# Expert stage of a vision tower kernel: both expert products in two row tiles of 64

## The reference

```
logits = x @ Wr.T                       # 16 experts
top_p, top_idx = top_k(softmax(logits), 2)
for each expert e:
    h   = gelu(x @ W1[e] + b1[e])       # 192 -> 768, "up"
    out = h @ W2[e] + b2[e]             # 768 -> 192, "down"
    y  += gate[e] * out
return x + y
```

## Time and profile before

| | us |
|---|---|
| median of 3 runs | 836.96 (836.1 to 840.61) |
| span of the profiled execution, first to last instruction | 860.4 |
| busy in it: PE | 726.7 |
| PEld | 609.2 |
| DVE | 408.3 |
| ACT | 371.2 |
| POOL | 348.5 |

### The profile page before, as it was taken

How to read it: one execution, slowest core, us unless ns; L and a number is a source line. 1 busy time by engine, 2 the same in 40 slices (tenths; PEclk the granted TensorE clock), 3 DMA queues, 4 the chain that set the end, 5 groups by cost and what they waited for, 6 DMA issues and landing times.

```text
span 860.4 us, 18555 instructions
## 1 busy us (share of the span) xinstructions
PE 726.7 (84%) x5774; PEld 609.2 (71%) x5774; DVE 408.3 (47%) x1214; ACT 371.2 (43%) x890; POOL 348.5 (41%) x534
## 2 busy tenths in 40 slices
PE   0409479999999999999853899999999999999990
PEld 0307356777677767676632799999999999999980
DVE  7001144688888888888765233222222222222228
ACT  0103225676666666666621333333333333333344
POOL 7740212357777777777675022122212212221220
PEclk9999558999999999999975899999999999999995
DMA  7710654444445544544061492645698778588249
GB/s 192 127 14 19 196 120 111 104 94 124 122 121 129 125 121 122 125 118 124 31 214 49 128 303 85 199 122 152 195 303 263 220 224 250 182 244 248 60 144 328
DMA packets 117226, 132.31 MB, mean 154 GB/s; under 512 B 18081, under 2 KB 102050, under 8 KB 116834
## 3 DMA queue, kind: packets, MB, share of 16 engines
q1 hardware_dynamic: 108434, 111.06, 46.9%
q0 software_dynamic: 8720, 20.36, 7.6%
HBM read 147.30 MB, written 35.49 MB: 212 GB/s over the span
## 4 chain that ended last, share of the span: by engine, by line
PE 58%; DVE 12%; issue 11%; POOL 9%; another core or an unknown queue 4%; ACT 2%; DMA 1%; SPq 1%; POOLq 1%; DVEq 0%; ACTq 0%
PE BK L451 18%; PE BK L436 13%; PE BK L441 8%; PE BK L707 4%; POOL slot_rows L1609 3%; PE BK L426 2%; PE BK L792 2%; PE BK L833 2%; POOL rs L1558 2%; DVE negmax L1322 2%; PE BK L812 2%; POOL hr L1598 1%; DVE hr L574 1%; PE BK L759 1%
## 5 line engine op out<-in xcount | busy, mean ns | idle before, releaser
L473 ACT ACTIVATE pixels<-BK,b1t 128x128 f32<-128x128 f32 x474 | 131.2, 375 | 241.8 <-PE BK L441 241.8
L585 POOL DMA_INDIRECT pair_rows<-shared x79 | 76.0, 962 | 294.0 <-DVE shared L551 289.5
L451 PE MATMUL BK<-shared,pixels 128*128 128x192 f32 x948 | 167.9, 325 | 0.0
L451 PEld LDWEIGHTS BK<-shared,pixels 128*128 128x128 f32 x948 | 153.0, 189 | 0.1
L1322 DVE TENSOR_REDUCE negmax<-BK 128x6 f32<-128x1536 f32 x64 | 112.5, 1757 | 25.0 <-PE BK L812 22.5
L436 PE MATMUL BK<-shared 128*128 128x128 f32 x948 | 120.0, 277 | 1.9 <-DVE shared L544 1.9
L436 PEld LDWEIGHTS BK<-shared 128*128 128x128 f32 x948 | 117.0, 193 | 2.8 <-DVE shared L544 2.8
L540 DVE TENSOR_TENSOR shared<-shared 128x1 int32<-128x1 f32 x79 | 12.6, 160 | 177.8 <-PE BK L427 175.6
L1113 ACT ACTIVATE shared<-BK 128x1536 f32<-128x1536 f32 x64 | 92.7, 1449 | 7.6 <-PE BK L833 6.7
L1609 POOL DMA_INDIRECT slot_rows<-xr,adr x64 | 64.8, 1013 | 36.5 <-issue 13.7
L441 PE MATMUL BK<-shared 64*128 64x128 f32 x948 | 74.9, 291 | 0.0
(11 more groups left out here) (202 smaller groups left out, 1087.9 us busy)
## 6 DMA issues: line engine op xcount, KB each, us to landing
shared<-ew SPq DMA_DIRECT2D x82, 576.0 KB
shared<-ew SPq DMA_DIRECT2D x82, 384.0 KB
shared<-up_rest SPq DMA_DIRECT2D x82, 192.0 KB
shared<-qk_parts SPq DMA_DIRECT2D x112, 96.0 KB
shared<-slot_rows SPq DMA_DIRECT2D x79, 104.0 KB
shared<-eb SPq DMA_DIRECT2D x82, 96.0 KB
qk_parts<-shared SPq DMA_DIRECT2D x32, 192.0 KB, 2.0
shared<-qk_parts SPq DMA_DIRECT2D x16, 288.0 KB
```

The source lines that it names most:

```text
L451: last = nc.tensor.matmul(Y[p], hT[p][:, c * P:(c + 1) * P], w2b[w][:, c, :], start=(c == 0), stop=(c == FC - 1))
L473: last = nc.scalar.activation(hT[p][:, c * P:(c + 1) * P], H[p][c], ACT.Gelu, bias=b1t[:, c, t:t + 1])
L585: nc.gpsimd.indirect_dma_start(pair_d, bass.IndirectOffsetOnAxis(t_dst[:, t:t + 1], 0), ysum[t % NB][:, :], None).then_inc(s[f"m_sc{t % NB ...
```

## The change

All PE work of the expert stage now uses 64 rows of the array at a time, alternating between the lower half (partitions 0 to 63, `LO`) and the upper half (`HI`).

- **Rows.** `rows_T` is four transposes of 64 rows by 128 features (features 0 to 127 and 64 to 191, for each half of the tile's rows) into two PSUM banks, one for each half of the array. The two banks now serve every tile, where before two tiles took turns. DVE copies them in three copies, the first of them 256 columns wide, so that the features lie in three slabs of 64: in the order 0, 1, 2 on the lower partitions and 1, 2, 0 on the upper ones.
- **Up.** The lower half of the array makes hidden chunks 0 to 2, the upper half chunks 3 to 5, each over three slabs: 18 products of 64 rows.
- **Down.** Each chunk of 128 hidden units is two products of 64 rows, the lower half summed in one PSUM bank and the upper in another: 12 products. DVE adds the bank of the lower half and the bias, waits for that, then adds the bank of the upper half. These two banks, too, serve every tile.
- **Weights.** The up weights are loaded straight from the input as two DMAs of 64 partitions x 3 slabs x 384. `st_up`, `up_rest` and the wait for them are gone.

```diff
 def rows_T(t):                                    # PE
-    p, r = t % 2, t % NB
+    r = t % NB
     pe.wait_ge(s[f"m_x{r}"], 16 * (t // NB) + 16)
-    wait_prev(pe, s["m_xT"], t - 1)
-    nc.tensor.matmul(XT[p][:, 0:P], xt[r][:, 0:P], ident[:, :], start=True, stop=True, is_transpose=True)
-    nc.tensor.matmul(XT[p][0:KR, P:2 * P], xt[r][:, P:E], ident[:, :],
-                     start=True, stop=True, is_transpose=True).then_inc(s["m_tr"], 1)
+    wait_prev(pe, s["m_xT"], t)
+    for f in range(2):
+        for h, k in enumerate((LO, HI)):
+            last = nc.tensor.matmul(XT[:, h, f, :], xt[r][k, f * RT:f * RT + P], ident[k, k],
+                                    start=True, stop=True, is_transpose=True)
+    last.then_inc(s["m_tr"], 1)
...
 def up(t):
-    for c in range(FC):
-        nc.tensor.matmul(H[p][c], w1a[w][:, c * P:(c + 1) * P], xtT[p][:, 0, :],
-                         start=(c % HC == 0), stop=False, skip_group_check=True)
     for c in range(HC):
-        for h in range(2):
-            k = slice(h * KR, (h + 1) * KR)
-            last = nc.tensor.matmul(H[p][h * HC + c], w1c[w][k, c * P:(c + 1) * P], xtT[p][k, 1, :],
-                                    start=False, stop=True, skip_group_check=True)
+        for k in range(NK):
+            for h, rows in enumerate((LO, HI)):
+                last = nc.tensor.matmul(H[p][h * HC + c], w1h[w][rows, (k + h) % NK, c * P:(c + 1) * P],
+                                        xtT[p][rows, k, :], start=(c == 0 and k == 0), stop=(k == NK - 1),
+                                        skip_group_check=True)
...
 def down(t):
-    wait_prev(pe, s["m_y"], t - 1)
+    wait_prev(pe, s["m_y"], t)
     for c in range(FC):
-        last = nc.tensor.matmul(Y[p], hT[p][:, c * P:(c + 1) * P], w2b[w][:, c, :],
-                                start=(c == 0), stop=(c == FC - 1))
+        for h, rows in enumerate((LO, HI)):
+            last = nc.tensor.matmul(Y[h], hT[p][rows, c * P:(c + 1) * P], w2b[w][rows, c, :],
+                                    start=(c == 0), stop=(c == FC - 1))
...
 def rows_T(t):                                    # DVE
-    V.tensor_copy(xtT[p][:, 0, :], XT[p][:, 0:P])
-    V.tensor_copy(xtT[p][0:KR, 1, :], XT[p][0:KR, P:2 * P])
-    V.tensor_copy(xtT[p][KR:P, 1, :], XT[p][0:KR, P:2 * P]).then_inc(s["m_xT"], 1)
+    V.tensor_copy(xtT[p][:, 0:2, :].rearrange("p s (h t) -> p s h t", h=2),
+                  XT[:, :, :, :].rearrange("p h s t -> p s h t"))
+    V.tensor_copy(xtT[p][LO, 2, :].rearrange("p (h t) -> p h t", h=2), XT[HI, :, 1, :])
+    V.tensor_copy(xtT[p][HI, 2, :].rearrange("p (h t) -> p h t", h=2), XT[LO, :, 0, :]) \
+        .then_inc(s["m_xT"], 1)
...
 def biased(t):
-    V.tensor_tensor(ysum[r][:, :], Y[p], b2b[w][:, :], ALU.add).then_inc(s["m_y"], 1)
+    V.tensor_tensor(ysum[r][:, :], Y[0], b2b[w][:, :], ALU.add).then_inc(s["m_yl"], 1)
+    dve.wait_ge(s["m_yl"], t + 1)
+    V.tensor_tensor(ysum[r][:, :], Y[1], ysum[r][:, :], ALU.add).then_inc(s["m_y"], 1)
...
 def first(t, e, new):                             # SP
-    sp.dma_start(w1a[w][:, :], ew1[ds(e, 1), 0:P, :].rearrange("a k f -> (a k) f"), cond=new) \
-        .then_inc(s[f"m_wa{w}"], 16)
-    sp.dma_start(w1c[w][:, :], w1c_d[ds(e, 1), :, :].rearrange("a k f -> (a k) f"), cond=new) \
-        .then_inc(s[f"m_wa{w}"], 16)
+    for h in range(2):
+        sp.dma_start(w1h[w][h * RT:(h + 1) * RT, :, :],
+                     ew1[ds(e, 1), :, h * (FF // 2):(h + 1) * (FF // 2)].rearrange("a (k r) f -> r (a k) f", r=RT),
+                     cond=new) \
+            .then_inc(s[f"m_wa{w}"], 16)
...
 def moe_loads(sp):
-    sp.wait_ge(s["st_w1c"], 32 * NE)
...
-            def st_up(e):
```

More of the change, by code:

```diff
@@ L69, in vit_tower @@
     qk_d = nc.dram_tensor("qk_parts", (2, 2, NPART, E, T), bf16).ap()
-    KR, HC = E - P, FC // 2
-    w1c_d = nc.dram_tensor("up_rest", (NE, P, FF // 2), fp32).ap()
+    RT, HC, NK = P // 2, FC // 2, 2 * E // P
+    assert NK * RT == E and NK == 3
     NW = 3
@@ L252, in vit_tower @@
         r_new = late([P, NTILE], i32)
-        w1a = [late([P, FF]) for w in range(NW)]
-        w1c = [late([P, FF // 2]) for w in range(NW)]
+        w1h = [late([P, NK, FF // 2]) for w in range(NW)]
         w2b = [late([P, FC, E]) for w in range(NW)]
@@ L260, in vit_tower @@
         t_dst = late([P, NTILE], i32)
-        xtT = [late([P, 2, P]) for p in range(2)]
+        xtT = [late([P, NK, P]) for p in range(2)]
         after_onehot = carve(pixels, n_pixels)
@@ L272, in vit_tower @@
         H = [[BK[:, 2 * p + c // HC, c % HC * P:(c % HC + 1) * P] for c in range(FC)] for p in range(2)]
-        XT = [BK[:, 4 + p, :] for p in range(2)]
-        Y = [BK[:, 6 + p, 0:E] for p in range(2)]
+        LO, HI = slice(0, RT), slice(RT, P)
+        XT = BK[:, 4:6, 0:P].rearrange("p h (s t) -> p h s t", s=2)
+        Y = [BK[:, 6 + h, 0:E] for h in range(2)]
         names = ("ld_const ld_idx0 ld_idx1 ld_idx2 ga0 ga1 ga2 dve_init pool_init act_xs "
@@ L282, in vit_tower @@
                  "r_dve r_diagd pe_row pe_tot r_tab "
-                 "m_x0 m_x1 m_x2 m_x3 m_wa0 m_wa1 m_wa2 m_wb0 m_wb1 m_wb2 m_b0 m_b1 m_b2 m_tr m_xT m_s1 m_gelu m_s2 m_y "
+                 "m_x0 m_x1 m_x2 m_x3 m_wa0 m_wa1 m_wa2 m_wb0 m_wb1 m_wb2 m_b0 m_b1 m_b2 m_tr m_xT m_s1 m_gelu m_s2 m_yl m_y "
                  "m_sc0 m_sc1 m_sc2 m_sc3 ld_p0 ld_p1 ld_p2 ld_p3 ld_p4 ld_p5 ld_p6 ld_p7 c_first c_out c_gated "
-                 "out_done st_w1c ld_b1 pe_b1 dve_b1 r_hot").split()
+                 "out_done ld_b1 pe_b1 dve_b1 r_hot").split()
         s = {n: sem(n) for n in names}
@@ L541, in rows_T @@
                 wait_prev(dve, s["m_s1"], t - 1)
-                V.tensor_copy(xtT[p][:, 0, :], XT[p][:, 0:P])
-                V.tensor_copy(xtT[p][0:KR, 1, :], XT[p][0:KR, P:2 * P])
-                V.tensor_copy(xtT[p][KR:P, 1, :], XT[p][0:KR, P:2 * P]).then_inc(s["m_xT"], 1)
+                V.tensor_copy(xtT[p][:, 0:2, :].rearrange("p s (h t) -> p s h t", h=2),
[3 more added lines that the diff above has]
+                    .then_inc(s["m_xT"], 1)
             def biased(t):
-                p, w, r = t % 2, t % NW, t % NB
+                w, r = t % NW, t % NB
                 dve.wait_ge(s["m_s2"], t + 1)
@@ L648, in ld_qk @@
                     at += nq
-            def st_up(e):
-                for h in range(2):
-                    sp.dma_start(w1c_d[ds(e, 1), h * KR:(h + 1) * KR, :].rearrange("a k f -> (a k) f"),
-                                 ew1[ds(e, 1), P:E, h * (FF // 2):(h + 1) * (FF // 2)].rearrange("a k f -> (a k) f")) \
-                        .then_inc(s["st_w1c"], 16)
             def step(i, p, on):
@@ L667, in step @@
                     a_mx(i, p, 1)
-                if on(1):
-                    st_up(i + 1)
             rows = g2_d.rearrange("(t g) (b c) -> b t g c", g=GP, c=C2)
@@ L693, in _ @@
             sp.dma_start(hrow[X0:X0 + T2, :, :], o2_d.rearrange("(b t) e -> t b e", t=T2)).then_inc(s["ld_o2"], 16)
-            assert NE == B
             over_images(sp, step, 0, 1, 3)
```

3 lines of the change are left out of this document (1 added, 2 removed).

## The result

The changed kernel takes 858.64 us (median of 4 runs, 855.69 to 861.59), the kernel before 838.79 on the same chip: ratio 1.0254, 95% interval 1.0230 to 1.0279. It is slower by about 20 us, where 28 less were forecast. One of the four runs behind the 838.79 took 1821.43 us; the other three have the median 836.96 given above, and against that the change costs 21.7.

The account below looks back on a forecast made before the run. PE was taken to bound the expert stage, with DMA the second limit. 32.2 us saved on PE, less 3 for DMA and 1.3 at the end, gave 27.9: from 836.96 to 809 us, own range 803 to 815, stated range 802 to 826.

Parts of the forecast that it names:

- PE's part: Expert stage on PE: a tile falls from 4.54 to 4.13 us, together 32.2 us less.
- the changeover: PE between 128-row and 64-row use: emptying and open weight loads leave 0.34 us of each tile without work.
- The rule that a weight load costs its columns whatever its rows: PE weight loads: in sequence, 60 would take 6.4 us a tile, the kernel some 980 us.
- rival C: PE in the expert stage cannot be fed so many short instructions: at 40 ns each, 882 us; chance 0.07.
- Rival A: PE at the groups' edges: part of the changeover stays, 825 us, or 833 if all stays; chance 0.14.
- DVE and the end: DVE's longer copy and second add lie beside PE, delaying nothing; after PE's last record, 1.3 us are added.
- Up weights straight from the input: Up loads and dropped copies: bytes and number of DMAs as before; taken as 0, between -2 and 0 us.
- What comes late next: DMA: Weight loads in long runs of new experts: 3 us lost, ends 0 and 11.6.
- Rival B: DMA takes the expert stage: 11.6 us lost instead of 3, 818 us; chance 0.14.
- S: Theory of the experiments, not the prediction: an up load of 64 partitions is slow wherever these lie.
- H: Theory of the experiments, not the prediction: up loads of 64 partitions come late, reaching only half the memory's ports.

Follow-up runs that it names:

- e1_noload: Changed kernel with the conditions of all expert-weight loads false, so only the first expert's weights are there: 834.62 us, ratio 0.9666 to the kernel before.
- e2_span128: Changed kernel with one up load of 128 partitions instead of two of 64, same 1536-byte pieces: 835.02 us, ratio 0.9656 to the kernel before.
- e4_slabcopy: Changed kernel with up weights copied into tile order during attention, then one load of 128 partitions a tile: 833.75 us, ratio 0.9652 to the kernel before.
- f4_down128: e4_slabcopy with down on 128 rows and one bias add, as before the change: 831.94 us, ratio 0.9945 to the kernel before.
- g3_twofull: e2_span128 with its up load cut into two by slabs, both over 128 partitions: 827.57 us, ratio 0.9889 to the kernel before.
- h2_before_regloads: Kernel before with two more register loads a tile in SP's list: 926.64 us, ratio 1.0729 to the kernel before.
- g4_actqueue: Changed kernel with the up load of partitions 64 to 127 issued by ScalarE instead of SP: 832.10 us, ratio 0.9946 to the kernel before.
- g1_nobias: Changed kernel without the per-tile loads of the second bias, the first expert's stays: 827.42 us, ratio 0.9893 to the kernel before.
- e3_long64: Changed kernel with both 64-partition up loads reading contiguous runs of 4608 bytes instead of 1536-byte pieces: 872.11 us, ratio 1.0097 to the kernel before.
- f3_mid64: e3_long64 with both up loads written to partitions 32 to 95, the second into another buffer: 847.47 us, ratio 1.0148 to the kernel before.
- h1_regloads: e2_span128 with two more register loads a tile in SP's list and no more transfers: 895.56 us, ratio 1.0399 to the kernel before.

## Why the prediction was wrong

**PE's part was right.** 4.13 us a tile were forecast and 4.14 are there; 32.2 us less for the stage, and without late weights it is 30.1 less (e1_noload) or 30.0 (e2_span128, e4_slabcopy). That the 0.34 us are the changeover is shown by f4_down128: half of the change alone, and the 0.34 a tile are back. That the sum agrees to 0.01 is luck in part: the transposes take the 0.12 of pairs, not the 0.15 taken, and down takes 2.02, not 1.97. The rule that a weight load costs its columns whatever its rows would have given 980 us; e1_noload excludes it as it excludes rival C: 64 loads and 64 matmuls in 4.14 us, one instruction per 32 ns, for the whole 220 us. Rival A fell as well, there is no gap at the groups' edges.

**DVE and the end were right or small.** The 256-wide copy takes 0.42 us for the 0.43 forecast, the adds 0.36 each:

```profile
575.44 0.36 DVE L556 TENSOR_TENSOR shared<-BK,shared 128x192 f32<-128x192 f32 x1 [0.92 <-PE BK L454]
...
577.64 0.42 DVE L545 COPY shared<-BK 128x256 f32<-128x256 f32 x1
```

The end was forecast 1.3 us longer and is not: 22.9 us in both.

**The step that failed is the supply of the weights**, two terms of the sum: "Up weights straight from the input", at 0, and "What comes late next: DMA", at 3, with ends 0 and 11.6. Both together measured 50.5 us. That is nearly the whole miss of 48.3 (27.9 less forecast, 20.4 more measured in the stage): 47.5 lie here and 2.1 in PE's gain, and the 1.3 of the end did not come. The bytes and the DMA share were weighed, and they do not decide: e2_span128 moves the same bytes in the same short pieces at a share of 1.01 without a gap. What was never added up is SP's list. Of the earlier trace rows only the lead was read, two tiles and 1.2 us, "then about 9.5 us", as if SP could start a load whenever a buffer came free. Measured, it is 6.7 us (median) after, and 9.4 in e4_slabcopy, where SP's list is short. SP's round stood in the timeline of SP behind the up load at 702.77 of the earlier trace rows:

```profile
707.75 0.09 SPq L362 DMA_DIRECT2D shared<-ew  x1
```

That is 4.98 us from one up load to the next, over PE's 4.54, and SP's 330.1 us of own time in the stage, 4.23 a tile, were above the 4.13 forecast for PE. So there are two parts:

- Even with the loads as they were, SP's list and the 13 to 20 us beside it would have held the stage at 343 to 350 us. That is 11 to 18 of the 50.5; the two full-height loads of g3_twofull, with 337.7 of own time, give 354.0. This part is an estimate, not a run: the kernel after with the old loads needs the old layout. h2_before_regloads fits it: 81.6 us more of own time (411.7 - 330.1) made the stage 62.4 longer, so the kernel before had 19 us to spare, and PE's gain asks for 30.
- The new loads made SP's list 35.4 us longer (365.5 - 330.1). The prediction's sentence was "Bytes and number of DMAs are as before". The number is, the issue is not. The view of one line, 560 to 780 us, shortest, median, longest in ns, before, and after:

```profile
L362 SPq DMA_DIRECT2D shared<-ew x48: 73/333/351, 561.5 to 776.1; - x48
```

```profile
L364 SPq DMA_DIRECT2D shared<-ew x87: 124/603/1145, 563.5 to 779.5; - x87
```

In a tile with loads the two up loads hold SP for 1.23 us (median of their sum) where they held it for 0.68. Over the 41 such tiles that is some 22.7 of the 35.4 us; the rest lies in held issues (9.6 against 3.8) and in small parts, down to the loads left out (0.12 against 0.07 at the shortest).

The Trainium skill, "Perfetto Trace Analysis", section "What "DMA-bound" means", lists the issuing engine's sequencer as a limit of its own beside the DMA engines; that is what the SP rows show here. The sign it gives, a track solid with DMA slices, is not there: the issues are 137 of the 365.5 us of SP's list, and the rest reads and handles registers. The Trainium skill, "DMA: Bandwidth & Descriptors", section "Issuing engines are not separate DMA queues", says that issuing from several engines only saves issue time, which is usually small beside the transfer. One issue is small here too (0.6 us, and 3.6 from its end to the last packet), but in a list that is too long the saving counts in every round: g4_actqueue gets 24.0 us of 382 by it. The Trainium skill, "DMA: Bandwidth & Descriptors", section "Rules for kernel authors", advises one transfer of 128 partitions over two to the halves, and e2_span128 against the changed kernel (332.0 against 382.4) agrees.

**The rivals.** Rival B named the place, waits of PE at L442 and L454 in the slices full of DMA, but by the wrong limit and so with the wrong size, 818. None of the cases was slower by this mechanism: the 0.07 for slower was rival C's, and the result came out slower for another reason. That the copies to `up_rest` cost nothing in attention was right, but they bought something: full-height loads. e4_slabcopy brings such a copy back, and has the forecast gain: 28.5 us under the kernel before, where 27.9 were forecast. That they are so near is luck in part, since the forecast had 2 us more for PE and took off 4.3 for DMA and the end.

**What stays open.** How much of the half-height loads' loss would be left if SP's time were free altogether: g4_actqueue and g1_nobias show a second limit at 358 to 359, in which transfers pile up behind their issues, and not what slows them (whether it is S or the ports of H). And why the issue of a half-height load takes 0.6 us: it is the same from ScalarE's queue (0.62), so it goes with the load's shape and not with SP's queue; longer pieces make it 0.47 to 0.53 (e3_long64, f3_mid64), full height 0.38 in pieces as short.

## What to carry to other kernels

Before a compute engine is made faster, add up the own time of the engine that issues its loads, over the whole stage and over the densest run: register reads and the issues themselves, skipped ones too. If its list per tile is longer than the new tile, it is the next bound, whatever the DMA share says; a loader whose view of waits is nearly empty, while its consumer waits, already is. Keep the number of loads per tile down and their height full, and pay for a layout that allows it in a stage where SP and DMA have time.

## What the runs showed of the hardware

- A value read into a register of SP costs 0.52 to 0.55 us: 156 of them made its list 85.9 us longer in h1_regloads (378.6 - 292.7) and 81.6 in h2_before_regloads (411.7 - 330.1).
- Issuing a load of 64 partitions holds the engine for 0.60 to 0.62 us in 1536-byte pieces; one load of 128 partitions with twice as many such pieces takes 0.38 (e2_span128).
- PE takes in 128 instructions in 4.14 us for 220 us on end (e1_noload).
- Going from half to whole rows of the array and back costs 0.34 us of a tile (4.48 in f4_down128 against 4.14).
- Packets of 4608 bytes take 300 ns (mean, e3_long64) where each load covers partitions 0 to 63 or 64 to 127, and 230 where it covers 32 to 95 (f3_mid64), without the stage being shorter.
